# Perceiver block on one core: four buffers for the first ropes, product sums kept in PSUM, three weight-sum instructions

## The reference

```
x = x + xattn(layernorm(x), ctx, ctx)   # 32 query heads, 8 key/value heads, head size 128, rope, causal
x = x + attn(layernorm(x))              # 32 heads of size 16, causal
x = x + ffn(layernorm(x))               # base product and a gated mixture of 8 rank-16 experts
```

```
rot = concatenate([-x2, x1])            # the two halves of the head size, exchanged
rope(x) = x * cos + rot * sin
```

## Time and profile before

| | before |
|---|---|
| median of three runs | 754.42 us |
| the profiled execution | 754.93 us |
| its span | 753.1 us, so 1.83 us lie around it |
| granted TensorE clock, mean | 0.989 |
| PE busy | 723.0 us, 96% |
| DVE, POOL, ACT busy | 538.8 us (72%), 494.4 us (66%), 376.6 us (50%) |

### The profile page before, as it was taken

One profiled execution on the slowest core, in us unless ns is written; L12 is line 12 of the kernel. 1 busy time (PEld: TensorE's weight loads), 2 busy tenths in 40 slices (PEclk: granted clock), 3 DMA queues, 4 the chain that ended last, 5 costly groups with the idle time before them and its releaser, 6 DMA issues.

```text
span 753.1 us, 12907 instructions
## 1 busy us (share of the span) xinstructions
PE 723.0 (96%) x4848; PEld 567.9 (75%) x4848; DVE 538.8 (72%) x830; ACT 376.6 (50%) x555; POOL 494.4 (66%) x367
## 2 busy tenths in 40 slices
PE   8999998599999999999999999979999999999897
PEld 6888876477877878778778778867776777777786
DVE  5756848876776867857858867666658877888855
ACT  5456545544644644744554546435246756653220
POOL 1897536687786877867967877736235798865350
PEclk9999999899999999999999999999999999999999
DMA  7554514031211310301211212101100010020002
GB/s 273 196 168 139 156 54 142 0 127 44 84 43 43 111 42 24 115 28 42 97 42 56 70 42 99 43 15 57 43 1 29 16 57 2 2 80 7 15 1 111
DMA packets 25561, 51.09 MB, mean 68 GB/s; under 512 B 2352, under 2 KB 10672, under 8 KB 25520
## 3 DMA queue, kind: packets, MB, share of 16 engines
q1 hardware_dynamic: 25520, 50.53, 20.2%
HBM read 40.04 MB, written 10.49 MB: 67 GB/s over the span
## 4 chain that ended last, share of the span: by engine, by line
PE 78%; DVE 10%; POOL 4%; ACT 4%; issue 3%; DMA 1%; SPq 0%; DVEq 0%; POOLq 0%; ACTq 0%
PE pj L1469 12%; PE pj L1562 10%; PE sc L1562 9%; PE tp L1469 7%; PE pj L1657 7%; PE pv L1455 5%; PE pv L1549 4%; PE sc L1529 4%; PE tp L1562 4%; PE tp L1443 2%; PE sc L1704 2%; PE tp L1717 2%; PE pj L1443 2%; PE pv L1728 2%; PE tp L1536 2%
## 5 line engine op out<-in xcount | busy, mean ns | idle before, releaser
L480 POOL TENSOR_TENSOR sw<-sw,cst 128x512 f32<-128x512 f32 x80 | 112.8, 1411 | 61.2 <-ACT sw L634 60.6
L1469 PE MATMUL pj<-x,w 128*128 128x512 f32 x384 | 104.2, 409 | 7.2 <-DVE cq L1044 5.2
L504 POOL TENSOR_TENSOR sm<-sm,mx 128x512 f32<-128x512 f32 x64 | 73.0, 1140 | 56.2 <-DVE mx L1132 36.3
L1469 PEld LDWEIGHTS pj<-x,w 128*128 128x128 f32 x384 | 69.4, 190 | 32.0 <-DVE cq L1044 12.6
L486 POOL TENSOR_TENSOR qr<-t,sw 128x512 f32<-128x512 f32 x59 | 82.3, 1396 | 10.2 <-DVE qr L1028 1.8
L498 POOL TENSOR_TENSOR w<-raw,w 128x896 fp32r<-128x896 f32 x28 | 60.2, 2172 | 37.7 <-ACT w L619 37.7
L745 ACT ACTIVATE sm<-sm 128x512 f32<-128x512 f32 x64 | 40.4, 631 | 84.4 <-POOL sm L504 84.3
L509 POOL TENSOR_TENSOR sm<-sm,rz 128x512 f32<-128x512 f32 x64 | 71.6, 1124 | 10.3 <-DVE rz L1138 10.3
L1469 PE MATMUL tp<-x,w 128*128 128x512 f32 x288 | 76.1, 400 | 0.1
L1000 DVE TENSOR_TENSOR t<-cq,cst 128x512 f32<-128x512 f32 x48 | 54.1, 1126 | 20.3 <-POOL qr L486 17.9
L1657 PE MATMUL pj<-xh,ws 128*128 128x512 f32 x192 | 66.3, 405 | 0.2 <-ACT kb L832 0.2
(11 more groups left out here) (251 smaller groups left out, 1782.5 us busy)
## 6 DMA issues: line engine op xcount, KB each, us to landing
rawd<-in_w_d SPq DMA_DIRECT2D x16, 512.0 KB, 3.3
raw<-in_w_q SPq DMA_DIRECT2D x15, 512.0 KB, 3.3
kscr<-sm SPq DMA_DIRECT2D x16, 256.0 KB, 2.2
vscr<-sm SPq DMA_DIRECT2D x16, 256.0 KB, 2.6
kr<-kscr SPq DMA_DIRECT2D x8, 512.0 KB, 3.3
vv<-vscr SPq DMA_DIRECT2D x16, 256.0 KB, 2.7
raw<-in_w_k SPq DMA_DIRECT2D x4, 512.0 KB, 6.2
cT<-in_ctxT SPq DMA_DIRECT2D x4, 512.0 KB, 7.4
```

The lines of the kernel that those rows point to most:

```text
L480: pool.tensor_tensor(bs(sw[par][:, :]), bs(sw[par][:, :]), rep(cst[:, C_SIN:C_SIN + S], HB), ALU.mult).then_inc(sin_done, 1)
L504: pool.tensor_tensor(s3, s3, per_group(mx[:, c, :], 8), ALU.subtract).then_inc(subbed, 1)
L1469: last = pe.matmul(bank, a, r, start=(start and k == 0 and part == 0), stop=(stop and k == 1 and part == 2), skip_group_check=True)
```

## The change

- The first eight ropes get four buffers per term: `t1f` is `t1` plus the two `pt` tiles, `swf` is `sw` plus the new `swx`. Their order is k = 0, 0, 1, 1, 2, 2, 3, 3 over the two pairs. POOL multiplies all eight by sin, adds numbers 0 to 3; DVE adds 4 to 7. Numbers 4 and 5 are added before 2 and 3. PE's first score product waits for four adds instead of five.
- On ACT `block_hi(4)` goes in front of the first two swaps.
- The sums for k = 0 and k = 3 are written back into bank C instead of `cq`. The swap then waits for the cos multiplication, as for k = 2, and PE's next product in bank C waits for the swap.
- PE's W_S2 no longer waits for `c_add` but for the copy of A, and the first products of a head's pair for the first half of the low weights alone.
- The weight sums take three instructions: 256, 512 and 256 columns, with blocks S2 and S3 exchanged in `raw8` (and both factors of the S3 product with the other sign).
- In head 0 DVE makes the weight sums of pair 3 before the third and fourth mask steps, and `wd_split(0)` behind the sum and cos step of k = 1.
- In head 6 `out_add(6, 4)` goes between the last two rope adds, and ACT's last swap in front of the last `c_hi`.

```diff
-        FIRST = [(0, 0), (1, 0), (0, 1), (0, 2), (1, 2), (1, 1), (0, 3), (1, 3)]
-        FIRST_DVE = (3, 5, 7)
+        FIRST = [(0, 0), (1, 0), (0, 1), (1, 1), (0, 2), (1, 2), (0, 3), (1, 3)]
+        t1f, swf = t1 + pt, sw + swx
 # POOL
-            for i, (p, k) in enumerate(FIRST):
-                rope_sin(i % 2, Q0 + i)
-                if i not in FIRST_DVE:
...
-                    rope_add(i % 2, Q0 + i, q_out(p, k))
+            for i in range(2):
+                first_sin(i)
+                first_add(i, i)
+            for i in range(2, 6):
+                first_sin(i)
+            first_add(2, 4)
+            first_add(3, 5)
+            first_sin(6)
+            first_sin(7)
 # ACT
-            swap_q(0, Q0, 0, cq[0], 1)
+            block_hi(4)
+            first_swap(0, C_BANK)
             v_copy(12)
-            swap_q(1, Q0 + 1, 0, cq[1], 2)
-            block_hi(4)
+            first_swap(1, T_BANK)
...
-            swap_q(0, Q0 + 2, 1, cq[0], 3)
-            swap_q(1, Q0 + 3, 2, A_BANK, None)
-            swap_q(0, Q0 + 4, 2, B_BANK, None)
+            first_swap(2, cq[0], 3)
+            first_swap(3, cq[1], 4)
+            first_swap(4, A_BANK, None, 1)
+            first_swap(5, B_BANK, None, 2)
             w7_hi(2, 0, raw8, 13)
...
+            first_swap(6, C_BANK, None, 5)
+            first_swap(7, T_BANK, None, 6)
...
-                    swap_q(k % 2, ri(2 * n + p, k), k, A_BANK if k == 2 else cq[j % 2], 6 * n + j + 1)
+                    swap_q(k % 2, ri(2 * n + p, k), k, (C_BANK, cq[p], A_BANK, C_BANK)[k], 6 * n + 3 * p + 2)
...
                 turn(1, 2)
+                if not more:
+                    turn(1, 3)
                 c_hi(q + 3, 3)
 # DVE
-                dve.tensor_tensor(b1, a21, a22, ALU.add).then_inc(wsum, 1)
-                dve.tensor_tensor(b3, a11, a21, ALU.subtract).then_inc(wsum, 1)
-                dve.tensor_tensor(b2, b1, a11, ALU.subtract).then_inc(wsum, 1)
-                dve.tensor_tensor(b4, a12, b2, ALU.subtract).then_inc(wsum, 1)
+                dve.tensor_tensor(raw[:, 4, :], raw[:, 0, :], raw[:, 3, :], ALU.add).then_inc(wsum, 1)
+                dve.tensor_tensor(raw[:, 5:7, :], raw[:, 0:5:4, :],
+                                  raw[:, 1, :].unsqueeze(1).to_broadcast([P, 2, 256]),
+                                  ALU.subtract).then_inc(wsum, 1)
+                dve.tensor_tensor(raw[:, 7, :], raw[:, 2, :], raw[:, 6, :], ALU.subtract).then_inc(wsum, 1)
...
-                dve.tensor_tensor(cq[par][:, :], bank, copy[:, :], ALU.add).then_inc(cadd, 1)
+                dve.tensor_tensor(bank if o is None else o[:, :], bank, copy[:, :], ALU.add).then_inc(cadd, 1)
...
                 t1_q(0, 0)
+                if first:
+                    w7_sum(3)
                 mask_max(q + 2, 2)
                 mask_max(q + 3, 3)
-                if first:
-                    w7_sum(3)
-                wd_split(g, 0, wdh, wdl)
+                if not first:
+                    wd_split(g, 0, wdh, wdl)
                 c_mix(0, 1)
                 t1_q(0, 1)
+                if first:
+                    wd_split(g, 0, wdh, wdl)
...
-                    for k in range(2, 4):
-                        rope_add_q(k % 2, ri(2 * n + 1, k), q_out(1, k))
+                    rope_add_q(0, ri(2 * n + 1, 2), q_out(1, 2))
+                    out_add(g, 4)
+                    rope_add_q(1, ri(2 * n + 1, 3), q_out(1, 3))
 # PE, in head
-                pe.wait_ge(rope, Q0 + 5 if first else ri(m, 0))
+                pe.wait_ge(rope, Q0 + 4 if first else ri(m, 0))
-                pe.wait_ge(wlo, 2 * m + 2)
+                pe.wait_ge(wlo, 2 * m + 1)
 # W_12:
-                pe.wait_ge(cadd, 3 * m)
+                pe.wait_ge(swp, ri(m, 0))
 # W_S2:
-                pe.wait_ge(cadd, 3 * m + 1)
+                pe.wait_ge(wlo, 2 * m + 2)
+                pe.wait_ge(pcp, 3 * m + 1)
 # W_S1:
+                pe.wait_ge(swp, ri(m, 0) + 1)
```

More of the change, by code:

```diff
@@ L50 @@
 LN_AT = 3
-W_11, W_12, W_22, W_S1, W_S2, W_S3, W_S4 = range(7)
+W_11, W_12, W_22, W_S1, W_S3, W_S2, W_S4 = range(7)
 X_11, X_21, X_22, X_T1, X_T2, X_T3, X_T4 = range(7)
@@ L94, in build @@
         sw = [sb(es, f"sw{i}", [P, HALF]) for i in range(2)]
+        swx = [sb(es, f"swx{i}", [P, HALF]) for i in range(2)]
         xs = ExitStack()
@@ L709, in swap_q, with first_swap @@
             def swap_q(par, n, k, src, ready):
-                if k == 2:
+                if k == 1:
+                    act.wait_ge(cadd, ready)
+                else:
                     act.wait_ge(t1_done, n + 1)
+                act.wait_ge(rope, n - 1)
+                swap(par, src)
+            def first_swap(i, src, ready=None, was=0):
+                if ready is None:
+                    act.wait_ge(t1_done, Q0 + i + 1)
                 else:
                     act.wait_ge(cadd, ready)
-                act.wait_ge(rope, n - 1)
-                swap(par, src)
+                act.wait_ge(rope, Q0 + was)
+                act.activation(swf[i % 4][0:64, :], src[64:128, :], ACT.Copy)
+                act.activation(swf[i % 4][64:128, :], src[0:64, :], ACT.Copy).then_inc(swp, 1)
             part_copy(pc, 1, A_BANK)
@@ L1037, in w7_lo, with c_add @@
                                   w7[p][:, 0, c].bitcast(F32), ALU.subtract).then_inc(wlo, 1)
-            def c_add(par, products, copies, was, bank, copy):
+            def c_add(products, copies, bank, copy, o=None):
                 dve.wait_ge(stp, products)
                 dve.wait_ge(pcp, copies)
-                dve.wait_ge(swp, was)
-                dve.tensor_tensor(cq[par][:, :], bank, copy[:, :], ALU.add).then_inc(cadd, 1)
+                dve.tensor_tensor(bank if o is None else o[:, :], bank, copy[:, :], ALU.add).then_inc(cadd, 1)
             piece_lo(0)
@@ L1084, in _ @@
             A2, C2 = B_BANK, T_BANK
-            dve.wait_ge(wlo, 4)
             for p, (c, copy) in enumerate(((C_BANK, pc), (C2, pcb))):
-                c_add(p, 2 + 2 * p, 1 + p, NKT, c, copy)
+                c_add(2 + 2 * p, 1 + p, c, copy)
                 dve.wait_ge(cadd, 1 + p)
-                t1_mul(p, Q0 + p, cq[p][:, :])
+                first_t1(p, c)
             block_lo(4)
@@ L1219, in head @@
                     w7_sum(2 * n + 3)
-                out_add(g, 4)
-                if more:
+                    out_add(g, 4)
                     out_add(g, 5)
@@ L1764, in _ @@
             pv_x(g, 0)
-            pe.wait_ge(cadd, 3 * N_PAIR)
+            pe.wait_ge(swp, Q0 + 8 * NKV)
             out_x(g - 1, 7, O6_BANK)
```

97 lines of the change are left out of this document (54 added, 43 removed).

## The result

The changed kernel took **746.24 us** (median of five runs, 745.94 to 747.20), the kernel before 754.42 (753.88 to 754.76). The ratio is 0.9896, 95% interval 0.9884 to 0.9907: 7.0 to 8.8 us faster. Forecast were 750.0 us and a range of 745.0 to 753.2. The sign and the range held; the size did not: 8.2 us came where 4.3 were summed. Some of that is not the change's: the two profiles are 8.7 us apart, and 7.4 of it arises between the first query product and head 7; 1.1 lies behind, in code that the change leaves alone.

A forecast was written before the change was run, and what follows sets the result against it. PE, 96% busy, bounds the kernel, with some 17 us of waits in one transient and one seam. Start 2.9, loop -0.6 and head 6 2.0 sum to 4.3 us, 750.6 by the profile; forecast 750.0, range 745.0 to 753.2.

The forecast's parts named there:

- The start: First ropes through head 0: 2.9 us gained is left of the start, ends 1.5 and 6.3.
- sin 2 at 116.8 pushes cos 3 to 117.35: First ropes: POOL's sine of number 2, ending at 116.8, delays the end of DVE's cos step 3 to 117.35.
- If add 4 does not have to stand behind sin 5: First ropes: under this condition PE's scores start up to 3.4 us earlier instead of 1.1.
- The lock: DVE and POOL: a two-input DVE step in SBUF and a POOL step do not run together; the later waits.
- end near 154.3: Head 0: POOL's low weights of pair 3 end near 154.3 instead of 155.30, after meeting both `wd_split` steps.
- I find it 0.6 us late at W_S1: Head 0, pair 3: the swap of k = 0 comes 0.6 us late for W_S1, cos being before swap.
- with no wait for `c_add`: Head 0, pair 3: W_S2 starts at 164.0 without waiting for the sum, against 167.52, 3.5 us earlier.
- Absorbed: Rival: one late chain takes over; start 1.5, end 1.2, loop 1.4 lost, 1.3 us gained, 753.1; chance 0.13.
- The loop: Loop of heads, `c_add` in PSUM: 0.2 us lost per head, 0.1 regained; balance 0.6 us lost, ends 0 and 1.4.
- Head 6: End of head 6, before head 7's scores: 2.0 us gained, ends 1.2 and 2.9.
- More: Rival: meetings of DVE and POOL mostly fall away; start 6.3, loop 0, end 2.7, so 9 us, 745.4; chance 0.16.
- C is held too long: Slower rival: dearer in-place sum or swap one ACT step later delays W_S1 and `u2` in seven heads, 756.5; chance 0.09.

The follow-up runs named there:

- e10: Changed kernel with the heads' sums in `cq` again, W_S2 still waiting for the copy `pc` alone, the sum's wait ahead of W_S1: 745.34 us.
- e12: Kernel before with one edit: W_S2 of both pairs waits for the copy `pc`, the wait for the sum moves to W_S1: 751.28 us, ratio 0.9959.
- e5: Changed kernel with all three sums of a head in `cq` as before, and W_S2 waiting for the sum of k = 0 again: 750.33 us.
- e1: Changed kernel with the end of head 6 as before (both last rope adds, `c_lo`, then `out_add`; ACT's last swap behind the last `c_hi`): 748.43 us.
- e7: Changed kernel with ACT's swap of k = 0 of the first pair put behind the second `wdh` copy in every head: 745.70 us.
- e2: Changed kernel with DVE's order in head 0 as before: weight sums behind the fourth mask step, `wd_split(0)` ahead of the k = 1 sum: 747.31 us.
- e9: Changed kernel with `u2` directly behind the swap, k = 0 cos step ahead of `sum_rec`, head 0's third exponential behind the copy `pc`: 745.85 us.
- e6: Changed kernel with the weight sums as four instructions of 256 columns each: 746.74 us.
- e15: Changed kernel, W_12 awaiting its own bank's swap, second low-weight half after last cos; from head 1 `u2` right after swap, cos before row sums: 744.87 us.

## Why the prediction was right in sign and short in size

**The start, forecast 2.9, measured 5.5.** This is the term that was mis-sized. By place, from the mark: third scores 3.65 (forecast 2.1), W_S2 of pair 3 5.5 (forecast 3.5), head 1 5.5 (forecast 2.9).
- "sin 2 at 116.8 pushes cos 3 to 117.35" did not happen. Cos 3 began 0.02 ahead of the sines and took 0.69; POOL's two sines took 3.09 instead of 2.6. So swaps 3 to 5 and the sines came earlier, the pair of sines 4 and 5 ended at 120.65 instead of 122.0. I also had add 4 behind sin 5; it ran beside it, from 119.51 on. Scores started at 122.46 instead of 124.0, the third product at 131.69 instead of 133.4. Some 0.5 of that 1.5 had come before: the first sum for k = 1 began at 113.01, not at 113.5. The forecast's own condition, "If add 4 does not have to stand behind sin 5", was the case; 2.4 of its "up to 3.4" came. The lock itself was read rightly, who holds it was not. The Trainium skill (SBUF — State Buffer, Who interferes with whom) says that the order of issue decides which of the two is blocked; cos 3 and the sines at 115.06 and 115.08 agree.
- POOL's low weights of pair 3, forecast to "end near 154.3", ended at 151.87 (145.72 plus 6.15). The chain behind them, by cos, swap, `c_hi` and `c_lo`, does release `out_x` 2 as forecast, but at 159.02 instead of 161.3, after a wait of PE of only 0.7.
- "I find it 0.6 us late at W_S1" did not happen either: the two rows 165.92 and 166.40 (transposes and W_S1) are 0.48 apart where e10 has 0.36, so 0.1 late.

The steps named came as named, only sooner: no wait for x above 0.2, W_22 at 143.93 (forecast 145.9) and at 1.66 us, W_S2 without a wait at 161.83 (forecast 164.0). The gains by part, each from undoing it at head 1, are 1.97 for `block_hi(4)` (forecast 1.7), 1.58 for four buffers, 0.79 for the order, 0.1 or less for the weight sums; with the 0.93 of W_S2's wait from e12 the sum is 5.3 of 5.5. That they add up is in part chance: beside the other parts W_S2's wait is worth 4.5 (e5 against e10), not 0.93, as the next paragraph shows.

**The most important part was costed as a detail.** W_S2 "with no wait for `c_add`" stood in half a sentence. Before, that wait was 0.97 us. But with the other parts PE reaches that point 4.6 us earlier, measured from the mark (72.6 in e5, 77.2 before), and the sum begins only 2.9 earlier (74.5 against 77.4), so the wait grows by the 1.7 between: e5 has it at 2.67, and with the low clock behind it 4.2 us are lost. That is what the rival "Absorbed" feared, one late chain that takes over, though by another chain than the one it named. It did not come since the change moved that very wait.

**The loop, forecast 0.6 lost, measured 0.2 won.** The mechanism was right, W_S1 and W_S3 late by the swap and `u2`, W_S2 less late. Both sizes were off: 0.2 lost is 0.29, since a short wait costs a restart of 0.14 as well; 0.1 regained is 0.32, for the same reason. The two cancel. A DVE write to PSUM in place took 0.692 on the mean, where 0.69 was forecast and 1.22 feared.

**Head 6, forecast 2.0, measured 1.8** (e1: 1.78). The row 493.01 shows what kept it from more: the add runs beside the last sine and takes 1.79.

**The rivals.** "More" came nearer than the forecast: 745.4 against 746.24. It had the start nearly (6.3 against 5.5) and the loop (0 against 0.2 won), not the seam (2.7 against 1.8); up to head 7 the profiles give 7.4 of its 9. Its reason was half right: cos steps from `cq` fell from 1126 to 822 ns. But the relief in the heads gave no time: e10 has 42 cos steps from `cq` at 1114 ns, and is no slower.

```profile
L1028 DVE TENSOR_TENSOR t<-cq,cst 128x512 f32<-128x512 f32 x42 | 46.8, 1114 | 20.5 <-POOL qr L488 18.4
```

The Trainium skill (GPSIMD Engine Reference, 8. Key points) puts contention on DVE instructions with two SBUF inputs; the traces agree, 686 ns from PSUM and 1114 from SBUF, and that changes no time in the loop, where PE is full. "C is held too long" was wrong in its trigger: the swap one ACT step later in the queue (e7) was not later in time. In head 0 the swap did hold W_S1 up, by 1.0 us at 138.24. Gains are absorbed in head 0 in e2 and e9 too. The tail's 1.1 us of the profiled span, a fall of the clock, was in no case: it is luck, and it brought the time nearer to "More".

## What to carry to other kernels

Ask of each wait on a full engine what it really protects: here one wait placed one product too early cost 2.5 us up to head 7 in the kernel before (2.0 to 4.2 by the times), and would have eaten half of what the change gives (750.33 in e5). A price of "one step later" holds only where the queue has no idle time ahead of the step, and one of the two longest waits in a table is worth 0.2 us at most if another chain ends 0.2 us before the same point. In a loop where PE is full, compare distances between starts, not the waits that are marked.

## What was not expected of the hardware

- A wait of PE of 0.11 to 0.16 us costs 0.25 to 0.31: the six matmuls behind it take 1.66 to 1.67 instead of 1.52 (rows at 301.87 and 325.64).
- A 2.72 us wait of PE left the scores behind it at full clock (granted 1.00; 2.08 us for 64 matmuls); behind the next, of 2.70 us, W_12 took 2.93 (clock 0.50) and the third scores 3.53 (0.56) instead of 2.08. In e10 the same third scores took 2.33 (0.99). The cost of the clock in such a transient is not fixed from one profile to the next, though the starts of the third scores agree within 0.1 us.
- Head 7's first scores follow a wait of 2.1 us in eleven profiles. In seven the clock then fell to 0.57 to 0.62 (mean of 4 us), in four (e6, e9, e10, e15) it stayed at 1.00. The wait of 1.77 us far behind them was followed by a low clock in nine of fourteen. Each fall costs 1.0 to 1.15 us. What decides was not tried; it can make two kernels differ by 0.15% that do the same.
